# Attention scores as fp32 products on two 32-row strips of TensorE, instead of bf16 parts

## The reference, cut to what matters

```python
h = _L0_tok_ref(x, dim_embedding, compatibility)
h = h + _L0_attn_ref(_layernorm(h), Wq, Wk, Wv, Wo)      # causal softmax
h = h + _L0_ffn_ref(_layernorm(h), ...)
h = h + _L1_attn_ref(_layernorm(h), Wq, Wk, Wv, Wo)      # causal, softmax over the 128 largest scores of a row
h = h + _L1_ffn_ref(_layernorm(h), ...)
# in both attentions: 32 query heads, 8 key/value heads, head width 32
scores = einsum("bkgtd,bksd->bkgts", rope(Q), rope(K)) / sqrt(32)
```

## Time and profile before

| | us |
|---|---|
| median of 3 runs | 5174.03 |
| the profiled execution's own time | 5178.51 |
| its span (first to last instruction) | 5176.7 |

### The profile page before, as it was taken

One profiled execution on the slowest core, in us unless ns is written; L12 is line 12 of the kernel. 1 busy time (PEld: TensorE's weight loads), 2 busy tenths in 40 slices (PEclk: granted clock), 3 DMA queues, 4 the chain that ended last, 5 costly groups with the idle time before them and its releaser, 6 DMA issues. The chain is left out here.

```text
span 5176.7 us, 79684 instructions
## 1 busy us (share of the span) xinstructions
PE 3755.9 (73%) x23338; PEld 2210.1 (43%) x23480; DVE 3509.0 (68%) x10383; ACT 3166.3 (61%) x7058; POOL 288.7 (6%) x213
## 2 busy tenths in 40 slices
PE   6998999998999999934555355555555555554699
PEld 2444766666444444412333233333333333332454
DVE  3654777776333356548888888888888888887444
ACT  1123777776000011259999599999999999999200
POOL 2332000000000023300000000000000000000000
PEclk9999999999999999966766566767766667766899
DMA  3325223232211112310111011110011110110222
GB/s 139 74 64 162 71 61 79 53 78 82 68 49 49 44 46 69 85 41 1 26 27 26 1 26 26 25 25 12 18 26 26 23 26 4 26 26 6 78 86 77
DMA packets 276875, 249.81 MB, mean 48 GB/s; under 512 B 170048, under 2 KB 209232, under 8 KB 276432
## 3 DMA queue, kind: packets, MB, share of 16 engines
q1 hardware_dynamic: 275888, 245.13, 18.0%
q0 software_dynamic: 544, 0.07, 0.0%
HBM read 167.56 MB, written 77.59 MB: 47 GB/s over the span
## 5 line engine op out<-in xcount | busy, mean ns | idle before, releaser
L1030 ACT ACTIVATE a_sign<-a_x,a_state 128x384 fp8e4<-128x384 f32 (+5 forms) x1536 | 1343.0, 876 | 126.3 <-DVE a_state L1166 87.9
L936 PE MATMUL a_ps_s<-k,q 128*128 128x512 bf16 (+3 forms) x1474 | 500.7, 486 | 692.0 <-DVE a_x L1267 661.7
L947 PE MATMUL a_ps_t<-ident,arena 128*128 128x128 f32 x2304 | 484.6, 355 | 194.3 <-ACT a_invT L999 130.6
L936 PEld LDWEIGHTS a_ps_s<-k,q 128*128 128x128 bf16 x1536 | 168.6, 131 | 916.3 <-DVE a_x L1267 749.8
L965 PE MATMUL a_ps_o<-a_probT,vals 128*32 128x128 f32 x4608 | 404.9, 325 | 185.1 <-ACT a_probT L995 184.7
L947 PEld LDWEIGHTS a_ps_t<-ident,arena 128*128 128x128 f32 x2304 | 338.6, 180 | 333.4 <-ACT a_invT L999 143.4
L721 ACT ACTIVATE a_prob<-a_x_neg,a_shift 128x640 f32<-128x640 f32 (+7 forms) x512 | 397.1, 776 | 80.4 <-DVE a_x_neg L764 61.9
L1267 DVE TENSOR_SCALAR_CACHE_REDUCE a_x<-a_ps_s 128x128 f32<-128x128 f32 (+7 forms) x512 | 383.7, 754 | 85.2 <-PE a_ps_s L939 59.9
L995 ACT COPY a_probT<-a_ps_t 128x512 f32<-128x512 f32 (+3 forms) x768 | 345.9, 475 | 111.1 <-PE a_ps_t L947 110.5
L764 DVE TENSOR_SCALAR_CACHE_REDUCE a_x_neg<-a_ps_s 128x640 f32<-128x640 f32 (+7 forms) x512 | 378.7, 751 | 38.8 <-PE a_ps_s L645 25.6
L1177 DVE MAX8 a_nine<-a_below 128x8 f32<-128x256 f32 (+6 forms) x448 | 371.0, 828 | 32.9
(11 more groups left out here) (216 smaller groups left out, 5947.7 us busy)
## 6 DMA issues: line engine op xcount, KB each, us to landing
q<-qk SPq DMA_DIRECT2D x256, 256.0 KB, 4.9
qk<-p_qkT SPq DMA_DIRECT2D x32, 960.0 KB, 6.2
h_rows<-h SPq DMA_DIRECT2D x32, 512.0 KB, 6.8
k<-qk SPq DMA_DIRECT2D x256, 64.0 KB, 5.2
m_o<-o SPq DMA_DIRECT2D x32, 512.0 KB, 5.5
m_h<-h SPq DMA_DIRECT2D x32, 512.0 KB, 5.3
h<-tok_h SPq DMA_DIRECT2D x16, 512.0 KB, 4.0
arena<-in_wo SPq DMA_DIRECT2D x16, 512.0 KB, 11.3
```

Source lines behind the costliest of these rows:

```text
L936: nc.tensor.matmul(ps_s[:, n % 2, a:a + w], q[:, y, head, i * P:(i + 1) * P], k[:, y, a:a + w], start=(y == 0), stop=False, skip_group_che ...
L947: mm = nc.tensor.transpose(ps_t[:, (n + 1) % 3, c:c + P], prob[:, par, at:at + P], ident[:, :])
L1030: ins = nc.scalar.activation(to, x[:, par, at:at + w], ACT.Sign, scale=-1.0, saturate=False, bias=state[:, par, 0, n:n + 1], accum_out=sta ...
```

## The change

The six bf16 products go. Queries and keys stay fp32 from the rotation on: GpSimd's block, the three parts and the bf16 identity of the projection go, ten fp32 transposes replace the thirty bf16 ones, in three turns with a bank each, and each turn waits only for its own third of the rotation. The DRAM copies have 1280 fp32 rows. A group's loads are 8 DMAs for queries and keys instead of 16.

The scores of a tile are two fp32 matmuls of K=32, one for each half of the keys. They use neighbouring 32-row strips of the array (`tile_position`) and write different PSUM banks. Even heads (in the second attention: even tiles) use strips 0 and 1, odd ones strips 2 and 3. In the first attention the strips 0 and 1 hold two of a group's four heads and strips 2 and 3 the other two; in the second attention every strip holds all four heads. The bias matmul stays a full bf16 one of K=128; for i=0 there are two of 64 columns. VectorE's fetch reads two banks with w/2 columns each.

```diff
-        TURNS = chunks(SPLITS * QK, 2 * BANK)
+        TURNS = chunks(QK)
...
                 def qk_transposes(j, par):
-                    pe.wait_ge(parts_ready, j + 1)
                     if not (isinstance(j, int) and j == 0):
                         pe.wait_ge(qkT_ready, j * NQ)
                     for t, (a, n) in enumerate(TURNS):
-                        if t >= 3:
-                            pe.wait_ge(qkT_ready, j * NQ + (t - 2))
+                        pe.wait_ge(rope_done, j * 3 + (t + 1))
                         for c in range(0, n, P):
-                            m = nc.tensor.transpose(ps_qk[:, t % 3, c:c + P], part[:, par, a + c:a + c + P],
-                                                    ident_b[:, :])
+                            m = nc.tensor.transpose(ps_qk[:, t, c:c + P], rot[:, par, a + c:a + c + P], ident[:, :])
...
-            @block.gpsimd
-            def _(pool):
...
                     if n == 0 and not (isinstance(j, int) and j < 2):
-                        dve.wait_ge(parts_ready, j - 1)
+                        dve.wait_ge(qkT_done, (j - 1) * NQ)
...
+    heads = qk_dram[ds(q_at, P), ds(t_at, T)]
+    for r in range(STRIPS):
+        rows = slice(r * DH, (r + 1) * DH)
+        mine = (heads.rearrange("(m d) t -> d m t", d=DH) if twice
+                else heads.rearrange("(y m d) t -> m d y t", m=2, d=DH)[r // 2])
+        sp.dma_start(q[rows, :, :], mine).then_inc(arrived, 16)
+        sp.dma_start(k[rows, :], qk_dram[ds(k_at, DH), ds(t_at, T)]).then_inc(arrived, 16)
+
+def head_scores(nc, ps, q, k, i, strips, ident_b, bias_b):
+    half = (i + 1) * P // 2
+    for a in range(2):
+        r = strips * 2 + a
+        rows = slice(r * DH, (r + 1) * DH)
+        nc.tensor.matmul(ps[:, a, 0:half], q[rows, i * P:(i + 1) * P], k[rows, a * half:(a + 1) * half], start=True,
+                         stop=False, tile_position=(r * DH, 0), skip_group_check=True)
+    for a in range(2) if i == 0 else (1,):
+        c, w = (0, half) if i == 0 else (half - P, P)
+        at = a * half if i == 0 else 0
+        last = nc.tensor.matmul(ps[:, a, c:c + w], ident_b[:, :], bias_b[:, at:at + w], start=False, stop=True,
+                                skip_group_check=True)
+    return last
...
-                        for a, w in chunks((i + 1) * P):
-                            for y in range(2):
-                                nc.tensor.matmul(ps_s[:, s % 2, a:a + w], q[:, x, y, m, i * P:(i + 1) * P],
-                                                 k[:, x, y, a:a + w], start=(y == 0), stop=False,
-                                                 skip_group_check=True)
-                        nc.tensor.matmul(ps_s[:, s % 2, i * P:(i + 1) * P], ident_b[:, :], bias_b[:, :], start=False,
-                                         stop=True, skip_group_check=True).then_inc(s_done, 1)
+                        head_scores(nc, ps_s[:, s % 2, :, :], q[:, x, m // 2, :], k[:, x, :], i, m % 2, ident_b,
+                                    bias_b).then_inc(s_done, 1)
...
-                        nc.vector.tensor_scalar(x_neg[:, c, 0:w], ps_s[:, s % 2, 0:w], -1.0, None, ALU.mult, ALU.min,
+                        nc.vector.tensor_scalar(x_neg[:, c, 0:w].rearrange("p (a c) -> p a c", a=2), ps_s[:, s % 2, :, 0:w // 2], -1.0, None, ALU.mult, ALU.min,
```

More of the change, by code:

```diff
@@ L266, in project @@
         v = sb("v", [P, 2, HKV * DH])
[L267 to L269 removed]
+        qkT = sb("qkT", [P, 2, QK])
         stats, mv, rstd = sb("stats", [P, 2, 12]), sb("mv", [P, 2, 2]), sb("rstd", [P, 2, 4])
@@ L390, in qk_evac @@
                         act.wait_ge(qkT_done, j * NQ + (t + 1))
-                        nc.scalar.copy(qkT[:, par, a:a + n], ps_qk[:, t % 3, 0:n]).then_inc(qkT_ready, 1)
+                        nc.scalar.copy(qkT[:, par, a:a + n], ps_qk[:, t, 0:n]).then_inc(qkT_ready, 1)
                 def step(j, par, first, last):
@@ L414, in _ @@
                 qk_evac(NT - 1, (NT - 1) % 2)
-            @block.gpsimd
-            def _(pool):
[L418 to L426, removed]
-                    nc.gpsimd.tensor_tensor(x, x, hi, ALU.subtract)
-                    pool.drain()
-                    nc.gpsimd.tensor_copy(mid, x)
-                    pool.drain()
-                    nc.gpsimd.tensor_tensor(lo, x, mid, ALU.subtract).then_inc(parts_ready, 1)
-                step(0, 0, True, False)
-                step(1, 1, False, False)
-                with pool.Fori(0, (NT - 4) // 2) as r:
-                    for c in (2, 3):
-                        step(r * 2 + c, c % 2, False, False)
-                step(NT - 2, 0, False, False)
-                step(NT - 1, 1, False, True)
             @block.vector
@@ L494, in _, with load_queries_keys @@
                 step(NT - 1, (NT - 1) % 2, False, True)
-def load_queries_keys(sp, gi, q, k, qk_dram, arrived, wait=None):
+def load_queries_keys(sp, gi, q, k, qk_dram, arrived, twice, wait=None):
     g, b = gi % HKV, gi // HKV
@@ L502, in load_queries_keys @@
         wait()
-    for x in range(2):
-        for r in range(4):
-            rows = slice(r * DH, (r + 1) * DH)
-            sp.dma_start(q[rows, x, :, :], qk_dram[ds(q_at + Q_PARTS[x][r] * QK, P), ds(t_at, T)].rearrange(
-                "(m d) t -> d m t", d=DH)).then_inc(arrived, 16)
-            sp.dma_start(k[rows, x, :], qk_dram[ds(k_at + K_PARTS[x][r] * QK, DH), ds(t_at, T)]).then_inc(arrived, 16)
+    heads = qk_dram[ds(q_at, P), ds(t_at, T)]
[18 more added lines that the diff above has]
+    return last
 def load_values(sp, gi, v, v_dram, arrived, wait=None):
@@ L928, in scores @@
                         if n == 0 and (1 - par) == 0:
-                            pe.wait_ge(qk_in, (s + 1) * 128 + 256)
+                            pe.wait_ge(qk_in, (s + 1) * 64 + 128)
                         if not (isinstance(s, int) and s < 0 and n < 2):
                             pe.wait_ge(x_ready, (s + 1) * (2 * TT) + (n - 1))
-                        head = ((1 - par) * 2) + m
-                        for a, w in chunks((i + 1) * P):
-                            for y in range(2):
-                                nc.tensor.matmul(ps_s[:, n % 2, a:a + w], q[:, y, head, i * P:(i + 1) * P],
-                                                 k[:, y, a:a + w], start=(y == 0), stop=False,
-                                                 skip_group_check=True)
-                        nc.tensor.matmul(ps_s[:, n % 2, i * P:(i + 1) * P], ident_b[:, :], bias_b[:, :], start=False,
-                                         stop=True, skip_group_check=True).then_inc(s_done, 1)
+                        head_scores(nc, ps_s[:, n % 2, :, :], q[:, (1 - par) * 2 + m, :], k, i, n % 2, ident_b,
+                                    bias_b).then_inc(s_done, 1)
                     def turn(n, m, i, a, w):
@@ L1950, in build @@
             same = Same(ident, causal, sb(now, "rope0", [P, 2, TT * 2 * DH]), same_in, 48)
-            q0, k0 = sb(now, "q0", [P, 2, 2, G, T], BF16), sb(now, "k0", [P, 2, 2, T], BF16)
+            q0, k0 = sb(now, "q0", [P, 2, G // 2, T]), sb(now, "k0", [P, 2, T])
             vals0 = sb(now, "vals0", [P, 2, TT * DH])
```

33 lines of the change are left out of this document (14 added, 19 removed).

## The result

The kernel after takes 5325.8 us (median of 4 runs, 5321.4 to 5330.3) against 5175.4 for the kernel before on the same chip: 1.029 times as long, interval 1.0275 to 1.031. That is 150 us slower; 117 were forecast. The profiled execution's span is 5328.5 us; before it was 5176.7.

| stretch, us | before | after | difference | forecast |
|---|---|---|---|---|
| start to first score | 476.4 | 449.1 | -27.3 | -29 |
| first attention, first score to last bias | 790.2 | 898.4 | +108.2 | +120 |
| from there to the second attention's first score | 970.7 | 943.1 | -27.6 | -29 |
| second attention, first score to last signs | 2554.0 | 2653.2 | +99.2 | +55 |
| the rest | 385.4 | 384.7 | -0.7 | 0 |

The account below looks back on a forecast made before the run. TensorE was taken to bound the projections and first attention; in the second attention it counts only where score tiles are waited for. Terms -58 + 120 + 55 = +117 us on 5174 gave 5291, say 5290; range 5150 to 5410.

Parts of the forecast that it names:

- Projections, -58: Both projections: fewer transposes save 1.19 us a tile, 36 us; shorter tails save 22; together 58 us saved.
- The change of array shape, 0.30 us a tile: Score tiles at 2.4 GHz: 0.10 us each to enter row strips, load the first weights and leave; bounds 0 to 0.41.
- rival 3: Score tiles: the two halves run one after the other, 246 us more in the first attention; about 5690 us; chance 0.03.
- First attention, +120: First attention: 157 us of added shape changes on TensorE, less 37 of idle time given back; bounds +57 to +210.
- the 37 that had names: First attention: TensorE's waits for exponentials, fetches and copies, 37 us by name, forecast to be given back as idle time.
- The bound of 100: First attention: lower bound of the loss, all 100 us of TensorE's idle time used up, leaving +57 us.
- rival 2: First attention: row strips lower the granted clock from 0.99 to 0.85, 140 us more, 5430 us; chance 0.10.
- Second attention, +55: Second attention: late score tiles 2 and 3 cost 1.6 us a slot, 50 us, plus 5 at the start; bounds +10, +90.
- One of my signs: Second attention: fetches of i = 2 and 3 would wait about 0.7 and 0.8 us instead of 0.67 and 0.40.
- covered fetches: Second attention, passes 0, 1 and 4: fetches are absent or behind masking work, which hides longer score tiles.
- Rival 1: Score tiles: shape changes are hidden, only the projections count, 5116 us; decides from below 0.14 us a tile; chance 0.13.

Follow-up runs that it names:

- The kernels with a tiny product: Kernel before plus one 16-column product ahead of each first-attention score tile: on one row strip 5248.3 us, over all 128 rows 5200.6 us.
- the control without any strip: Kernel before plus a 16-column product over all 128 rows, no tile position, ahead of each first-attention score tile: 5200.6 us, +27.8 against before.

## Why the prediction came out as it did

**Projections, -58; measured -54.9.** The step stands. From the first tile's transposes to the last but one's, 14 steps, TensorE took 331.15 us before (123.43 to 454.58) and takes 315.10 now (124.31 to 439.41): 16.1 us, 1.15 a step where 1.19 were forecast. My row was not quite typical, since in every second tile of before the product behind the transposes starts 0.24 us earlier than in it. The forecast multiplied by 15; the fifteenth turns beside the last tile's rotation and saves nothing of its own. The tail was 10.3 us shorter (forecast 11) and store and loads 1.8 (counted at nothing). Against them, the first transposes stand 0.9 us later, because the passes at the projection's beginning ran at 1.06 us, 1.2 GHz, until about 84.3 us where before it was 82.5. That is 27.3; the second projection gives 27.6.

**The change of array shape, 0.30 us a tile.** The step stands, in each part: 0.09 to enter (0.10), 0.10 for the first pass, whose load lies open (533 ns from first to second pass for 512 columns, 427 without it), 0.09 to leave, 0.01 before the transposes. At 1.2 GHz entering cost 0.14 (0.351 for 0.213 us), the first pass 0.16, leaving 0.14, as I had them from the token map. The Trainium skill, "TensorEngine Tiling (Array Packing)", section "Key Properties", says the engine drains at a change of mode; the way back from row strips, which no row of before showed, now agrees with it. Strips' first passes start 6 to 8 ns apart in all 512 tiles, which ends rival 3.

**First attention, +120; measured +108.** The work term was right (512 x 0.30), two others were not and nearly cancelled, so that this stretch came out within 12 us is in part luck. Idle time gave back about 75 us (154 of work and 29 of clock, below, less the 108), not the 37 that had names. The rest I had left in place as latency of semaphores and seams; TensorE's named waits at ScalarE and VectorE shrank from 36 us to 2.4 (2.3 of my 37 were the row's "issue", a wait without a name), and the unnamed gaps with them. The bound of 100 was nearer than the sum of the names. Against that, the granted clock fell from 0.99 to 0.96. That was rival 2 in small: the trace has seven drops to 0.5 of 6.8 or 10.2 us, before two of 3.4, some 25 us by the work they halve, and at the stage's start the full clock comes 14.1 us after the first score where it came after 5.5, another 4 us. Five of the seven stand at the loop's seams, where TensorE stands still for 1.8 to 2.4 us:

```profile
909.35 1.09 PE L641 MATMUL a_ps_t<-ident,a_prob 128*128 128x128 f32 x8 [2.36 <-ACT a_prob L702]
910.37 2.08 PE L486 MATMUL a_ps_s<-k,q 32*128 32x512 f32 x4
912.37 0.29 PE L491 MATMUL a_ps_s<-a_bias_b,a_ident_b 128*128 128x128 bf16 x1
```

The row-strip passes at 910.37 and the transposes after them take double. The kernels with a tiny product show drops at their seams too (five each), the control without any strip as well. So strips are not needed for a drop. Nor does the standstill alone decide: before, TensorE stood still for 2.3 to 3.0 us at five seams and the clock fell at two. Why there are more drops than before is open.

**Second attention, +55; measured +99.** The mechanism and its size hold: 48 in the slots (50) and 10.6 at the start (5), by the pair of kernels without exact selection. By a slot's waits it is 0.30 + 0.41 = 0.71 in pass 2 (the forecast's 0.74, which counts tile 2's delay in), the same in pass 3 and 0.19 there at the widest tile: 1.61, as forecast. ScalarE's waits for a threshold grew by as much, 19 us in all slots at the start of pass 3 and 28 at that of pass 4. One of my signs did not fit my own sum: a wait of 0.67 and 0.30 more is 0.97 at i = 2, not 0.7; it is 0.98. TensorE's added work at i = 4 and 5 is free, as the step said of covered fetches. What is missing from the sum is the exact selection, +41 us: a branch on data, for which the prediction has no step. It put at nothing what the change does to the rows that need it; the new scores are not the same bits as the old, and I take it that the search, which stops by counting, misses its count on another row for that reason. The trace of before had the price (one slot of 134 us among those of 78), so the question could have been asked. With other data it may fall the other way.

**The range and the rivals.** 5326 lies in the stated range, 36 above the forecast. The stretches missed by +44 in the second attention, -12 in the first and +3 in the projections; the 44 are mostly the exact selection's, for which there was no term, and that they did not lead out of the range is luck. Rival 1, hidden changes of shape, needed under 0.14 us a tile; there are 0.30. Its first sign would have been waits that shrink by what the tiles add; the second attention's grew.

## What to carry to other kernels

A change of the array's shape is a fixed price for each visit, so count visits, not columns: here 0.30 us for 1,024 tiles on the path or near it outweighed a projection 27 us shorter, twice. Before you fill or lengthen a wait, ask at which hand-over it ends: 0.6 us of waits filled from within a pass counted in full, and 1.15 us brought in from the next pass to fill 0.98 gained nothing. Count first how long the engine behind the hand-over waits: here it was 12 us where 44 of waits stood. Batching two pieces to save a switch takes two buffers at once, and with two buffers it turns overlap into turns. And a change that alters rounding can alter which branches run: look for them before you compare times.

## What the hardware showed that I had not expected

A product of 16 columns in a strip costs TensorE 0.20 us in all, some seven times its 0.03 over the full array. Four row strips with work of two tiles give the time of one (0.44 us for eight passes of 128 columns). In the kernel after, each of five standstills of TensorE of 1.8 to 2.4 us at the loop's seams came with 6.8 or 10.2 us at the lower clock; before, of five of 2.3 to 3.0 us only two did, with 3.4. The Trainium skill, "TensorE: Matmul & The Clock Gate", section "What's actually happening", lets sustained busy time release the clock; that fits the ends of these drops, where TensorE was busy (from 909.35 us on without a pause, for one), while the token map's stretch at 1.2 GHz still does not, and nothing run here explains it.
